# Feed-forward of a fused decoder layer: the order of Vector's single-column operations

## What is computed

```python
def rms_norm(x, g):
    var = jnp.mean(x * x, axis=-1, keepdims=True)
    return x * jax.lax.rsqrt(var + EPS) * g

def activation_quant(x):
    scale = 127.0 / jnp.clip(jnp.max(jnp.abs(x), axis=-1, keepdims=True), 1e-05, None)
    return jnp.clip(jnp.round(x * scale), -128, 127) / scale

def bit_linear(x, w, g):          # weight_quant(w): rounded to -1, 0, 1 times one scale
    xn = rms_norm(x, g)
    return activation_quant(xn) @ weight_quant(w).T

y = bit_linear(x, gate_w, gate_norm_w)     # 512 -> 2 * 1408
gate, up = jnp.split(y, 2, axis=-1)
h = gate * sigmoid(gate) * up
return bit_linear(h, down_w, down_norm_w)  # 1408 -> 512
```

## Time and profile before

| | |
|---|---|
| median of three runs | 1101.44 us |
| the profiled execution's own time | 1103.72 us |
| its span in the profile | 1101.7 us |
| PE busy | 1014.1 us (92%) |
| PEld busy | 773.2 us (70%) |
| DVE busy | 799.5 us (73%), 1447 instructions |
| ACT busy | 672.4 us (61%), 1220 instructions |
| POOL busy | 622.1 us (56%), 604 instructions |

### The profile page before, as it was taken

How to read it: one execution, slowest core, us unless ns; L and a number is a source line. 1 busy time by engine, 2 the same in 40 slices (tenths; PEclk the granted TensorE clock), 3 DMA queues, 4 the chain that set the end, 5 groups by cost and what they waited for, 6 DMA issues and landing times.

```text
span 1101.7 us, 25335 instructions
## 1 busy us (share of the span) xinstructions
PE 1014.1 (92%) x9636; PEld 773.2 (70%) x9636; DVE 799.5 (73%) x1447; ACT 672.4 (61%) x1220; POOL 622.1 (56%) x604
## 2 busy tenths in 40 slices
PE   4689999999999999999998789999999998699996
PEld 4577778888888888888876567766767765344443
DVE  6578776656666566677767667878887866799995
ACT  5544654544545454455576258777777756688785
POOL 2664675657656567565678445645454535555552
PEclk9789999999999999999999989999999998899999
DMA  9125452424232332424466678687887642000001
GB/s 340 71 98 209 180 206 103 166 91 153 95 136 103 130 119 111 154 103 179 157 229 160 165 169 188 174 192 180 181 191 171 132 101 58 10 30 29 30 30 39
DMA packets 51145, 147.69 MB, mean 134 GB/s; under 512 B 10448, under 2 KB 24272, under 8 KB 39760
## 3 DMA queue, kind: packets, MB, share of 16 engines
q1 hardware_dynamic: 42432, 87.32, 29.6%
q0 software_dynamic: 8064, 58.72, 14.4%
q10 hardware_dynamic: 528, 0.00, 0.0%
HBM read 120.46 MB, written 25.17 MB: 132 GB/s over the span
## 4 chain that ended last, share of the span: by engine, by line
PE 56%; issue 11%; DVE 11%; POOL 9%; DMA 6%; ACT 5%; SPq 1%; POOLq 0%; DVEq 0%; ACTq 0%
PE Qb L233 4%; PE Qb L235 4%; PE Qb L234 4%; PE XY L1078 4%; PE Yb L318 4%; PE Yb L320 4%; PE Yb L319 4%; POOL x_hg L1485 3%; DMA x_K<-k_parts 3%; PE Sm L1016 3%; PE Se L1024 3%; PE Sm L1024 3%; PE Se L1016 2%; DVE a_turned L702 2%; POOL a_ql L570 2%
## 5 line engine op out<-in xcount | busy, mean ns | idle before, releaser
L1654 DVE TENSOR_REDUCE x_mx<-Sm 128x4 f32<-128x768 f32 x128 | 122.3, 955 | 63.2 <-PE Sm L1024 62.2
L233 PE MATMUL Qb<-a_xTh,WqH 128*128 128x256 f32 x512 | 147.0, 287 | 3.9 <-DVE a_vl L762 3.7
L234 PE MATMUL Qb<-a_xTl,WqH 128*128 128x256 f32 x512 | 146.3, 286 | 0.0
L235 PE MATMUL Qb<-a_xTh,WqL 128*128 128x256 f32 x512 | 146.2, 285 | 0.0
L588 POOL TENSOR_TENSOR a_pr<-a_pr_plain,a_ph 128x512 fp32r<-128x512 f32 x64 | 83.5, 1305 | 104.4 <-ACT a_ph L403 104.4
L702 DVE TENSOR_TENSOR a_turned<-Qb,sinS 64x512 f32<-64x512 f32 (+1 forms) x144 | 94.9, 659 | 60.0 <-PE Qb L235 43.7
L570 POOL TENSOR_TENSOR a_ql<-a_rot,a_qh 128x512 fp32r<-128x512 f32 x64 | 84.0, 1317 | 95.8 <-ACT a_qh L423 95.6
L415 ACT ACTIVATE Lb<-Lb 128x512 f32<-128x512 f32 x64 | 37.2, 582 | 164.2 <-PE Ob L305 164.2
L1252 ACT ACTIVATE x_ex<-Se 128x768 f32<-128x768 f32 x128 | 103.9, 812 | 52.9 <-PE Se L1024 52.7
L318 PE MATMUL Yb<-a_WoH,a_oH 128*128 128x512 f32 x256 | 103.8, 405 | 2.8 <-POOL a_oN L566 2.7
L233 PEld LDWEIGHTS Qb<-a_xTh,WqH 128*128 128x128 f32 x512 | 99.6, 194 | 7.7 <-issue 3.2
(11 more groups left out here) (211 smaller groups left out, 2805.0 us busy)
## 6 DMA issues: line engine op xcount, KB each, us to landing
a_WoH<-wo_parts POOLq DMA_DIRECT2D x28, 1024.0 KB, 5.2
a_WoL<-wo_parts POOLq DMA_DIRECT2D x28, 1024.0 KB, 7.1
x_K<-k_parts SPq DMA_DIRECT2D x32, 256.0 KB, 7.6
q_parts<-x_qp SPq DMA_DIRECT2D x16, 384.0 KB, 3.0
k_parts<-x_kp SPq DMA_DIRECT2D x16, 384.0 KB, 3.6
x_Q<-q_parts SPq DMA_DIRECT2D x16, 384.0 KB, 5.5
a_w_stage<-in_gateT SPq DMA_DIRECT2D x8, 704.0 KB, 4.1
x_w_stage<-in_gateT SPq DMA_DIRECT2D x8, 704.0 KB, 4.8
```

The costliest lines, as they stand in the source:

```text
L233: pe.matmul(out, w_hi(k), xTh[:, k, :], start=(k == 0), stop=False)
L234: pe.matmul(out, w_hi(k), xTl[:, k, :], start=False, stop=False)
L235: mm = pe.matmul(out, w_lo(k), xTh[:, k, :], start=False, stop=(k == KD - 1))
L1654: dve.tensor_reduce(mx[:, half, at:at + 4].rearrange("p (j a) -> p j a", j=2), Sm[:, :, 0:2 * WIN].rearrange("p j (a c) -> p j a c", a=2), ...
```

## The change

Only Vector's program changes, and two small buffers.

- `rows_scale` is cut into four functions: `rows_maximum` (amax), `rows_bound`, `rows_inverse`, `rows_scale` (ascale). rows_maximum(b+3) is now issued in step b right after rows_weighted(b+3), at the end of the step; the other three stay in the step after, for b+2.
- `hidden_scale` is cut into hidden_bound, hidden_inverse and hidden_scale. After h(b, 0) the order becomes hbound, bound, hinv, binv, hscale, ascale.
- `first_squares` is gone. `ss` has a fourth column that is set once to the constant term, and `mean_square` is one reduction over the four columns, now ahead of `whole_maximum`.

```diff
-    ss = sb("ss", [P, NC], F32)
+    ss = sb("ss", [P, NC + 1], F32)
...
-    hsum, hms, rms = sb("hsum", [P, 1], F32), sb("hms", [P, 1], F32), sb("rms", [P, 1], F32)
+    hms, rms = sb("hms", [P, 1], F32), sb("rms", [P, 1], F32)
...
-    sb("keys_end", [P, KEYS_END], F32)
+    sb("keys_end", [P, KEYS_END + 8], F32)
...
-        def first_squares(b):
-            wait(dve, ss_ready, NC * b + 2)
-            wait(dve, hms_ready, b)
-            dve.tensor_scalar(hsum[:, :], ss[:, 0:1], ss[:, 1:2], EPS / 127.0 ** 2, ALU.add, ALU.add).then_inc(hsum_ready, 1)
-
         def mean_square(b):
-            wait(dve, hsum_ready, b + 1)
-            wait(dve, ss_ready, NC * b + 3)
+            if b == 0:
+                wait(dve, term_set, 1)
+            wait(dve, ss_ready, NC * (b + 1))
             wait(dve, rms_ready, b)
-            dve.tensor_tensor(hms[:, :], hsum[:, :], ss[:, 2:3], ALU.add).then_inc(hms_ready, 1)
+            dve.tensor_reduce(hms[:, :], ss[:, :], AX.X, ALU.add).then_inc(hms_ready, 1)
...
         def ffn_step(b):
             if real(b - 1):
                 hidden_maximum(b - 1, 2)
+                mean_square(b - 1)
                 whole_maximum(b - 1)
-                mean_square(b - 1)
             if real(b):
                 hidden(b, 0)
+            if real(b - 1):
+                hidden_bound(b - 1)
+            if real(b + 2):
+                rows_bound(b + 2)
+            if real(b - 1):
+                hidden_inverse(b - 1)
+            if real(b + 2):
+                rows_inverse(b + 2)
             if real(b - 1):
                 hidden_scale(b - 1)
             if real(b + 2):
...
                 hidden_maximum(b, 0)
                 hidden(b, 2)
                 hidden_maximum(b, 1)
-                first_squares(b)
             if real(b + 3):
                 rows_weighted(b + 3)
+                rows_maximum(b + 3)
...
             dve.reciprocal(w_inv[:, :], w_mean[:, :]).then_inc(constants_ready, 1)
+            dve.memset(ss[:, NC:NC + 1], EPS / 127.0 ** 2).then_inc(term_set, 1)
...
         rows_weighted(2)
+        rows_maximum(2)
         residual(B - 2)
```

More of the change, by code:

```diff
@@ L981, in cross_and_ffn @@
     gu_full, silu_ready, h_ready = sem("gu_full"), sem("silu_ready"), sem("h_ready")
-    ss_ready, hsum_ready, hms_ready, rms_ready = sem("ss_ready"), sem("hsum_ready"), sem("hms_ready"), sem("rms_ready")
+    ss_ready, term_set, hms_ready, rms_ready = sem("ss_ready"), sem("term_set"), sem("hms_ready"), sem("rms_ready")
     hg_ready, hparts_ready, hidden_link = sem("hg_ready"), sem("hparts_ready"), sem("hidden_link")
@@ L1763, in rows_weighted, with rows_maximum @@
                                      op0=ALU.subtract, op1=ALU.mult).then_inc(xg_ready, 1)
-        def rows_scale(b):
-            scale = t["scale"][:, b:b + 1]
+        def rows_maximum(b):
             wait(dve, xg_ready, b + 1)
@@ L1769, in rows_scale, with rows_bound, rows_inverse @@
             dve.tensor_reduce(amax[:, :], xg[:, :], AX.X, ALU.max, apply_absolute_value=True).then_inc(row_link, 1)
+        def rows_bound(b):
             wait(dve, row_link, 2 * b + 1)
-            wait(dve, row_link, 2 * b)
             wait(dve, f1_ready, b)
             wait(dve, n_step, 5 if b < FIRST else 10)
-            dve.tensor_scalar(bound[:, :], amax[:, :], scale, EPS, ALU.mult, ALU.max).then_inc(bound_ready, 1)
+            dve.tensor_scalar(bound[:, :], amax[:, :], t["scale"][:, b:b + 1], EPS, ALU.mult, ALU.max).then_inc(bound_ready, 1)
+        def rows_inverse(b):
             wait(dve, bound_ready, b + 1)
@@ L1777, in rows_scale @@
             dve.reciprocal(binv[:, :], bound[:, :]).then_inc(row_link, 1)
+        def rows_scale(b):
             wait(dve, row_link, 2 * b + 2)
             wait(dve, xr_ready, b)
-            dve.tensor_scalar(ascale[:, :], binv[:, :], scale, 127.0, ALU.mult, ALU.mult).then_inc(ascale_ready, 1)
+            dve.tensor_scalar(ascale[:, :], binv[:, :], t["scale"][:, b:b + 1], 127.0, ALU.mult, ALU.mult).then_inc(ascale_ready, 1)
         def rows_quantised(b):
@@ L1819, in whole_maximum, with hidden_bound, hidden_inverse @@
             dve.tensor_reduce(hmax[:, :], hparts[:, :], AX.X, ALU.max).then_inc(hidden_link, 1)
-        def hidden_scale(b):
+        def hidden_bound(b):
             wait(dve, hidden_link, 2 * b + 1)
             wait(dve, rms_ready, b + 1)
-            wait(dve, hidden_link, 2 * b)
             wait(dve, f2_ready, b)
             dve.tensor_scalar(hbound[:, :], hmax[:, :], rms[:, 0:1], 127.0 * EPS, ALU.mult, ALU.max).then_inc(hbound_ready, 1)
+        def hidden_inverse(b):
             wait(dve, hbound_ready, b + 1)
@@ L1829, in hidden_scale @@
             dve.reciprocal(hinv[:, :], hbound[:, :]).then_inc(hidden_link, 1)
+        def hidden_scale(b):
             wait(dve, hidden_link, 2 * b + 2)
@@ L1964, in _ @@
         rows_weighted(0)
+        rows_maximum(0)
+        rows_bound(0)
+        rows_inverse(0)
         rows_scale(0)
@@ L1968, in _ @@
         rows_weighted(1)
+        rows_maximum(1)
+        rows_bound(1)
+        rows_inverse(1)
         rows_scale(1)
```

## The result

The changed kernel took a median of 1109.09 us (1108.28 to 1110.36, four runs) against 1101.64 for the kernel before (four runs): ratio 1.0061, interval 1.0044 to 1.0078. It is slower. On a second chip it was 1106.16 (six runs) against 1100.75 (fifteen): 1.0044, interval 1.0031 to 1.0056. The two intervals overlap from 1.0044 to 1.0056, 4.9 to 6.2 us. The profiled span is 1107.0 us, 5.3 more.

A forecast was written before the change was run, and what follows sets the result against it. Scalar's serial chain was taken to hold part A and Vector alone part B. 6.27 - 0.33 + 0.38 - 0.14 - 0.24 = +5.94 us on 1101.44 gave 1107.4 us, range 1101.0 to 1110.5 (main case 1104.5 to 1109).

The forecast's parts named there:

- Part A: Feed-forward step from H, start of h(b,0) on Vector, to start of h(b,1): held by Scalar's chain, 4.13 to 4.10 us.
- hq's wait: In part A on Vector: hq, free at H + 2.06, waits for Scalar's hr until H + 2.93.
- Part B: Start of h(b,1) to the next H, set by Vector alone: the moved amax adds 0.57 us a step.
- xg's end: Part B on Vector: xg ends 0.55 us behind GpSimd's x_hg pair, so the removed first_squares gives back nothing.
- Part A of the eleven steps: Part A summed over steps 2 to 12: 11 x -0.03 = -0.33 us.
- Steps 0 and 1: First two steps: 2 x 0.57, less 0.36 of idle time and 0.40 of L1814 being held: +0.38 us.
- The end: Step 13 without amax, -0.14 us, and the last step with mean_square's reduction in front, about -0.24.
- The alternation: Part A on Vector: interleaving the hidden and rows' chains saves 0.42 us of latency, which turns into waiting.
- Rival 1: Part A: alternated independent operations don't overlap, Scalar's chain 0.38 us longer in 12 steps, 1112 us; chance 0.07.
- Rival 2: Part A: only hq's wait binds, silu not late for h(b,1); part A 3.79, total 1103.9 us; chance 0.07.
- Rival 4: Stage runs at Vector's issue rate, -0.64 us a step, capped by TensorE at 2.95: at best 1098.5 us; chance 0.10.

The follow-up runs named there:

- after_again: The changed kernel, unaltered, run again beside the kernel before on a second chip: 1106.16 us against 1100.75, ratio 1.0044.
- maximum_between: The changed kernel with the rows' maximum put back beside Scalar's chain, between hbound and bound in the alternated order: ratio 1.0069 to the kernel before.
- after_silu_first: The changed kernel with Scalar's silu of chunk 1 issued ahead of the rounding of rows xr: ratio 1.0026 to the kernel before.
- combined: Kernel before with one-reduction mean_square ahead of whole_maximum, X between the rows' maximum and bound, silu of chunk 1 ahead of xr: 1095.73 us against 1102.39, ratio 0.9948.
- residual_between: Kernel before with one-reduction mean_square ahead of whole_maximum and X between the rows' maximum and bound, silu not moved: 1103.36 us, one run.

## Why the prediction was right

The forecast was 1107.4, +5.94 us; the two comparisons gave +7.45 (1109.09) and +5.41 (1106.16), and both intervals hold 5.94. Point by point:

- *Part A, 4.13 to 4.10*: 4.09. hq's wait was put at 0.87 and is 0.80, as hr starts at H + 1.42 and hq at H + 2.90; h(b,1)'s at 0.31 and is 0.29.
- *Part B, +0.57 a step*: 4.57 to 5.15, +0.58. xg's end, reckoned from GpSimd's pair, was right to 0.01 us. Summed over steps 2 to 12 part B grew from 51.63 to 57.66, by 6.03; with 0.35 of issue wait that the kernel before had once and the changed one hadn't, 6.38, against 6.27.
- *Part A of the eleven steps, -0.33*: -0.10, since in step 4 binv waited 0.26 on issue and pushed hscale and hr behind it; -0.39 without it. after_again has the same wait.
- That the eleven steps together, +5.93, meet the forecast's 6.27 - 0.33 = 5.94 to 0.01 is partly luck: the 0.35 that the kernel before waited and the 0.29 by which step 4 is longer now were not foreseen, and they nearly cancel.
- *Steps 0 and 1, +0.38*: from the third xg to H of step 2, 22.21 became 22.61, +0.40.
- *The end, -0.38*: from H of step 13 to the span's end 37.78 became 37.50, -0.28; the program's last matmuls took 4.2 us in both.
- Sum: 0.40 + 5.93 - 0.28 = 6.05, against 5.94 forecast. The span grew by only 5.3 because the stage happened to be reached 0.75 earlier in this execution.
- *The alternation saves 0.42 of latency*: it saves more (hbound to X is 0.69; I had 0.73), all of it turned into waiting.
- *Rival 1*, that independent operations don't overlap: they start 0.08 to 0.13 apart where dependent ones took 0.20 and 0.24. The Trainium skill (VectorE: DVE Perf Modes, section "The DRAIN you can't avoid") says that the next operation waits for an empty pipeline, but adds that a next operation that is not held starts earlier. The prediction took the first half alone; the trace agrees with the second: bound starts 0.12 behind hbound, which lasts 0.20. But the mechanism by which rival 1 would have cost time is real: maximum_between makes hscale 0.72 later and pays 0.68.
- *Rival 2* (only hq's wait binds) is what after_silu_first builds: 3.71 in part A, where the rival had 3.79.
- *Rival 4* (Vector's issue rate is the bound) fell with the 0.80 and 0.29 us for which Vector stands idle in part A. Its ceiling was wrong: 97.01 - 94.06 = 2.95 us was to be all that TensorE leaves, but combined's eleven steps are 3.56 shorter. Busy time by modelled ends is no floor; what stops combined is the loop of 8.47 a step.

What I got wrong was smaller. I took the removed operation and the reordered mean_square for one edit worth 0.14 in the last steps and nothing in the others, because part B's sum hid it: without the reordering the step would have been 9.42, and the whole about 11 x 0.18 = 2 us worse. The change is thus two: the reordering, -0.18 a step; and the moved maximum, +0.72. The expectation for residual_between failed on the point that the forecast had got right for the change itself: who waits for the operation that comes later.

Left open: why the first medians are 7.4 us apart and the second 5.4. The stage explains 6, and an offset of 1 to 2 us may come from the stages before and from the last matmuls (below), which differ from run to run.

## What to carry to other kernels

An engine that is busy without a gap is not yet the bound: lay the timelines of two engines over each other from one common release, and see which chains end together. Work that lies beside another engine's chain is free there and costs its full time wherever it is moved; shortening latency inside such a stretch only lengthens the wait at its end. Before an operation is put off, look for who waits for its result on an in-order queue, and what stands behind it there.

## What the runs showed of the hardware

- xg, a Vector operation with two inputs in SBUF, is held up while a product runs on GpSimd. It takes 0.74 us alone, 0.86 when it starts 0.31 before GpSimd's end, 0.98 when 0.43 before, 1.77 and 1.75 for the third xg of the two traces, and each time ends 0.55 behind GpSimd. The wait is not shown as idle time but as a longer duration, so where one operation's duration varies from place to place, look for a wait in it. The Trainium skill (SBUF — State Buffer, section "SBUF: two separate sides") has an exclusive port for this pair of operations, by which the later one is blocked fully. The trace agrees that xg waits for GpSimd's end, but not for all of its 0.74: only 0.55 follows that end.
- Vector's single-column operations start 0.08 to 0.13 us apart when independent, 0.20 (behind a reciprocal) or 0.24 apart when each needs the one before.
- The last eleven matmuls of the program (L1203), which run alone after 1.44 us of waiting, took 4.2 us in the profiled executions of before and after and 2.55 in that of after_again, and up to 4.9 in others. The tables of stages for these stretches, before and after_again:

```profile
1094.20:1098.40 4.20, 4.20 (x11) 1.30 (x11) 0.00 (x0) 0.00 (x0) 0.00 (x0) 0.59 0.00 0
```

```profile
1100.50:1103.10 2.60, 2.52 (x11) 1.00 (x11) 0.00 (x0) 0.02 (x1) 0.00 (x0) 1.00 0.00 0
```

The granted clock is 0.59 on average in the one and 1.00 in the other, that is, partly at the lower of the two levels, 1.2 and 2.4 GHz. What TensorE did before was the same in the changed kernel and in after_again: waits of 1.90, 1.97 and 1.44 us between its last groups of matmuls. The difference moves the end by 1.7 us, as much as three steps of the change, and from a single execution it can't be told from the effect of an edit.
